# Moving the product of open attention steps ahead of a step's other VectorE work, and their bounds to GpSimd

## What is computed

```python
x = x + attn(layernorm(x)); x = x + ffn(layernorm(x))
# attn, 16 heads of 16
q_h, k_h, v_h = exp_map(q), exp_map(k), exp_map(v)          # points in the Poincare ball
diff  = |q_h|^2 - 2 q_h.k_h + |k_h|^2
denom = max((1 - c|q_h|^2) * (1 - c|k_h|^2), 1e-5)
arg   = max(1 + 2c * diff / denom, 1 + 1e-5)
w     = softmax(-beta * arccosh(arg) / sqrt(c))
out   = exp/log maps of (w @ log_map(v_h)), then @ W_o.T
# ffn: x scaled and cast to float8_e4m3, matmul with an equally cast kernel, bias
```

## Time and profile before

| what | us |
|---|---|
| median of 3 runs | 1977.56 |
| lowest, highest | 1976.21, 1979.98 |
| the profiled execution's own time | 1984.73 |
| its span, first to last instruction | 1982.9 |
| ScalarE busy | 1867.4 (94%) |
| TensorE busy | 1759.5 (89%) |
| VectorE busy | 1146.3 (58%) |
| GpSimd busy | 12.9 (1%) |
| mean granted TensorE clock | 0.974 |

### The profile page before, as it was taken

The page is one execution under the profiler, slowest core; times in us unless marked ns, Lnnn a source line. Parts: engine busy times, 40 slices in busy tenths (PEclk is TensorE's granted clock), DMA queues, the critical chain, the costliest instruction groups (busy, mean ns, idle before and its releaser), DMA issues.

```text
span 1982.9 us, 29304 instructions
## 1 busy us (share of the span) xinstructions
PE 1759.5 (89%) x10579; PEld 577.9 (29%) x10579; DVE 1146.3 (58%) x2855; ACT 1867.4 (94%) x1094; POOL 12.9 (1%) x35
## 2 busy tenths in 40 slices
PE   7989989899898798989898898998989899899896
PEld 4322222222222222222222222222222222223234
DVE  7555565655656656565656656556565655513545
ACT  5899999999999699999997899999999999999993
POOL 2000000000000000000000000000000000000000
PEclk9899999999999899999998899999999999989998
DMA  1322222041403114032040320414032031401110
GB/s 56 113 95 65 89 102 75 23 134 44 134 22 102 53 44 133 23 102 75 23 133 22 102 75 27 129 43 134 22 102 76 23 123 43 124 22 43 43 54 23
DMA packets 112952, 142.52 MB, mean 72 GB/s; under 512 B 35691, under 2 KB 61548, under 8 KB 112748
## 3 DMA queue, kind: packets, MB, share of 16 engines
q1 hardware_dynamic: 112748, 140.13, 22.8%
HBM read 85.07 MB, written 55.05 MB: 71 GB/s over the span
## 4 chain that ended last, share of the span: by engine, by line
ACT 53%; PE 24%; issue 14%; DVE 6%; ACTq 2%; DMA 0%; DVEq 0%; SPq 0%
ACT U L1217 27%; ACT U L1224 25%; PE ps L1100 8%; PE ps L402 7%; PE ps L1115 6%; ACTq L1265 2%; DVE U L1294 1%; PE ps L407 1%; DVE U L1285 1%; PE ps L698 0%; PE ps L1138 0%; ACT e L530 0%; DVE rows L555 0%; DMA U<-in_L_attn_W_o_dram 0%; DVE rp L624 0%
## 5 line engine op out<-in xcount | busy, mean ns | idle before, releaser
L1224 ACT ACTIVATE U<-U 128x2048 f32<-128x2048 f32 x512 | 1003.1, 1961 | 0.3
L1217 ACT ACTIVATE U<-ps 128x2048 f32<-128x2048 f32 x500 | 961.9, 1924 | 29.0 <-PE ps L1100 26.8
L1100 PE MATMUL ps<-q_T,k_T 18*128 18x512 f32 x4096 | 635.9, 650 | 150.2 <-ACT U L1217 113.1
L1115 PE MATMUL ps<-U,vals 128*32 128x512 f32 x4096 | 559.4, 619 | 25.7 <-ACT U L1224 24.7
L1100 PEld LDWEIGHTS ps<-q_T,k_T 18*128 18x128 f32 x4096 | 199.8, 186 | 377.4 <-ACT U L1217 316.8
L402 PE MATMUL ps<-wT,xnT 128*128 128x384 f32 x512 | 228.4, 538 | 1.9 <-ACT xnT L463 1.9
L491 DVE COPY qkv<-ps 128x384 f32<-128x384 f32 x112 | 62.5, 558 | 244.2 <-PE ps L402 244.2
L1115 PEld LDWEIGHTS ps<-U,vals 128*32 128x32 f32 x4096 | 81.5, 109 | 200.9 <-ACT U L1224 168.2
L402 PEld LDWEIGHTS ps<-wT,xnT 128*128 128x128 f32 x512 | 79.4, 190 | 193.4 <-issue 121.1
L407 PE MATMUL ps<-ident,rows 128*128 128x128 f32 x512 | 107.6, 308 | 15.9 <-DVE rows L555 13.1
L407 PEld LDWEIGHTS ps<-ident,rows 128*128 128x128 f32 x512 | 55.0, 147 | 193.6 <-issue 132.6
(11 more groups left out here) (210 smaller groups left out, 1181.6 us busy)
## 6 DMA issues: line engine op xcount, KB each, us to landing
rqb<-q_scratch SPq DMA_DIRECT2D x64, 1024.0 KB, 5.6
q_scratch<-q_T SPq DMA_DIRECT2D x16, 1024.0 KB, 4.5
k_scratch<-k_T SPq DMA_DIRECT2D x16, 1024.0 KB, 7.2
v_scratch<-vals SPq DMA_DIRECT2D x16, 768.0 KB, 4.2
fi_xt<-in_L_attn_x_dram SPq DMA_DIRECT2D x17, 512.0 KB, 5.7
xt<-in_L_attn_x_dram SPq DMA_DIRECT2D x15, 512.0 KB, 6.4
out_dram<-fi_x SPq DMA_DIRECT2D x15, 512.0 KB, 4.2
rk_scratch<-rk SPq DMA_DIRECT2D x16, 32.0 KB, 8.8
```

Of the source, the lines that this page charges most:

```text
L1100: ins = pe.matmul(g.ps[:, 2 * pair + i, :], a.k_T[HB * h:HB * h + RD, b % 2, hg, kt * P:(kt + 1) * P], a.q_T[HB * h:HB * h + RD, G % 3, hg ...
L1115: ins = pe.matmul(g.ps[HB * h:HB * h + VW, 6, :], a.vals[:, b % 2, kt, (hg * HPG + h) // 2, DH * (h % 2):DH * (h % 2) + VW], U[:, n % RING ...
L1217: act.activation(U[:, n % RING].rearrange("p b n -> p (b n)"), chunk(n), ACT.Ln, scale=-2.0 / EPS, bias=1.0).then_inc(freed, 1)
L1224: act.activation(U[:, n % RING], U[:, n % RING], ACT.Exp, scale=exponent).then_inc(exp_done, 1)
```

## The change

GpSimd now walks the 128 units with a branch of its own. In an open unit it makes the bounds of the four steps (four instructions of 128x512 each), each step as soon as its `U` buffer is free; in a closed one it adds to `m_rdy`. VectorE no longer makes bounds. Its pieces are written as `rest(n)` and now run one step later in its stream: the product of step n, then the pieces of n-1. The flag of the next unit is loaded into a register at the last step of a unit, ahead of the pieces of the step before, and only the branch stays at the unit's head. In the tables A0 goes from slot 27 to slot 26 and A1 from slot 31 to slot 32, with R1, R2, R5 and R6 whole or split to fit; in slot 25 `amax` comes ahead of the scaling of the k rows. TensorE's and ScalarE's code is otherwise the same.

```diff
-                ("R", 0): (25, BOTH), ("R", 1): (26, BOTH), ("R", 2): (27, 0), ("A", 0): (27, 1),
-                ("R", 3): (28, BOTH), ("R", 4): (29, BOTH), ("R", 5): (31, 0), ("A", 1): (31, 1),
-                ("R", 6): (32, BOTH), ("R", 7): (33, BOTH)}
+                ("R", 0): (25, BOTH), ("R", 1): (26, 0), ("A", 0): (26, 1), ("R", 2): (27, BOTH),
+                ("R", 3): (28, BOTH), ("R", 4): (29, BOTH), ("R", 5): (31, BOTH),
+                ("R", 6): (32, 0), ("A", 1): (32, 1), ("R", 7): (33, BOTH)}
...
         if k == 25:
+            v.tensor_reduce(amax[:, :], a4[:, :, :].rearrange("p t h -> p h t"), AX.X, ALU.max).then_inc(amax_rdy, 1)
             scale_rows(v, n, (1,))
-            v.tensor_reduce(amax[:, :], a4[:, :, :].rearrange("p t h -> p h t"), AX.X, ALU.max).then_inc(amax_rdy, 1)
...
+                def bound(n):
+
+                    G, hg, kt = split(n)
+                    if n >= RING:
+                        pool.wait_ge(pv_done, n - RING + 1)
+                    for h in range(HPG):
+                        ins = pool.tensor_scalar(U[:, n % RING, place(n, h), :], rqb[:, h, :],
+                                                 a.rk[:, (G // 2) % 2, hg * HPG + h, kt:kt + 1],
+                                                 1.0 / EPS, ALU.mult, ALU.min)
+                    ins.then_inc(m_rdy, 1)
+
+                for n0 in range(0, N, UNIT):
+                    o = opened(n0)
+                    pool.wait_ge(a.open_rdy, flags_of(n0))
+                    hold(pool, passed_pool)
+                    is_open = pool.value_load(a.opens[0:1, o:o + 1], min_val=0, max_val=1)
+                    with pool.If(is_open > 0):
+                        pool.wait_ge(rqb_in, 16 * (n0 // KT + 1))
+                        for n in range(n0, n0 + UNIT):
+                            bound(n)
+                    with pool.Else():
+                        if n0:
+                            pool.wait_ge(m_rdy, n0)
+                        pool.sem_inc(m_rdy, UNIT)
...
-                        if is_open and n + 1 < n0 + UNIT:
-                            bound(n + 1)
-                            clamp(n + 1)
...
+                def unit(n0, products):
+
                     for n in range(n0, n0 + UNIT):
...
+                        if products:
+                            clamp(n)
+                        if n == n0 + UNIT - 1 and UNIT <= n < N - 1:
+                            load_flag(n + 1)
+                        if n:
+                            rest(n - 1)
+                        if n == UNIT - 1:
+                            load_flag(n + 1)
```

## The result

| | before | changed |
|---|---|---|
| median of 10 runs, us | 1983.38 | 1992.88 |
| lowest, highest | 1976.21, 1989.13 | 1992.45, 1997.40 |
| the profiled execution | 1984.73 | 1992.56 |
| its span | 1982.9 | 1990.7 |

The changed kernel is slower: ratio 1.0046, 95% interval 1.0028 to 1.0064. The forecast was 32.5 us faster, with a range of 1939 to 1958 us. The time moved the other way. Of the 47.8 us between the forecast and the measured median 5.8 are this difference of the starting point; the other 42.0 are the change, 32.5 of gain that did not come and 9.5 of loss.

The account below looks back on a forecast made before the run. ScalarE, busy 94%, was taken to bound the kernel. Gains of 13.5 + 12.0 + 2.7 + 4.3 = 32.5 us off a median of 1977.56 gave 1945.1 us, main range 1939 to 1953, 8 in 10 range 1939 to 1958.

Parts of the forecast that it names:

- What bounds the kernel: ScalarE, busy 94% of the span, sets the pace; reordering other engines can only take back its idle time.
- the bound on GpSimd: Open units: 0.8 us assumed per bound of 512 elements, costing nothing up to 1.18 us because the ring covers it.
- The fourth rival: The change does nothing: bounds take about 2 us each, only the closed-unit gain is left; 1973 to 1978 us, chance 0.04.
- the slower rival: GpSimd's bounds decide the open units: slower from 2.05 us each, 2023 us at 3 us each; chance 0.06.
- Terms 1 and 2: First and second open units: earlier products cut ScalarE's waits for products and distances; gains 13.5 and 12.0 us.
- Halved waits for distances: Beside the open units, ScalarE's waits for distances of 2.6, 1.9 and 0.7 us fall to 1.3, 1.0 and nothing.
- Term 3: Third open unit: without bounds on VectorE every product is early, so waits of 2.0 and 0.7 us go; gain 2.7 us.
- Term 4: Closed units, branch at s 20: moved branch and earlier flag load remove three ScalarE waits for distances; gain 4.3 us.
- Edits at nothing: Other unit heads, A0 a step earlier, bursts of `rqb` loads and GpSimd's closed-unit branches were expected to cost nothing.
- The first: Rival: waits return inside the open units as copies behind the product delay TensorE's fill and next distances; 1956.5 us, chance 0.10.
- The second: Rival: TensorE's idle time ahead of R0 goes but one ahead of A0 comes, no closed-unit gain; 1949.4 us, chance 0.08.
- The third: Rival: VectorE pieces with two SBUF inputs wait for GpSimd bounds in units one and two, 5 us; 1950 us, chance 0.06.

Follow-up runs that it names:

- e5: Kernel before plus 32 extra GpSimd instructions of several forms behind the last values, to price them; the bounds' form took 1.99 us, no kernel time given.
- e4: Changed kernel with two heads of each open step bounded by GpSimd and two by VectorE; 1961.45 us, ratio to before 0.9887.
- e8: Changed kernel with GpSimd only multiplying, by tensor_tensor, and the minimum taken in VectorE's product; 1966.88 us, ratio to before 0.9925.
- e1: Changed kernel with the bounds back on VectorE, each step's four just ahead of its product; 1969.0 us, ratio to before 0.9927.
- e6: e2 with the first product of a unit behind the pieces, as in the kernel before; 1970.83 us, ratio to before 0.9939.
- e7: e4 with the slots of the kernel before; 1963.64 us, ratio to before 0.9900.
- e9: e8 with the slots of the kernel before for R1, A0, R2, R5, A1, R6; 1969.29 us, ratio to before 0.9930.
- e2: e1 with the slots of the kernel before for R1, A0, R2, R5, A1, R6; 1964.31 us, ratio to before 0.9917.

## Why the prediction was wrong, point by point

**What bounds the kernel** held: ScalarE is at 94% in every version, and the result followed its waits.

**The step that failed** is the bound on GpSimd, taken at 0.8 us from a memset and a select, with both ends of its range (0.45 and 1.18) below the 1.99 measured. Neither of those rows does what a bound does. The kernel before had a GpSimd tensor_scalar, the 16 instructions of L359 at 388 ns each, which the prediction doesn't use. With 16 elements a row it is nearly all fixed cost by e5's line (0.29 us fixed) and could not have given the price of 512; that had to be measured. e5 shows the form itself to be dear. The threshold that I had worked out, 1.19 us each for the first unit to be covered, was not measured itself, but fits: GpSimd spent 1.04 us per head and step in e4 and 0.98 in e8, and no product waited for it; at 2.03 eleven of twelve did.

**The fourth rival** described what came in units one and two: with 1.96 us as the price at which nothing changes, their waits rose by 1.1 and 1.3 us only. It had a chance of 0.04. Its arithmetic for the third unit, and that of the slower rival, was wrong: I gave all three units the 31.3 us of the first. In the second and the third, the values that free the first buffer and the fourth product stood like this in the kernel before:

```profile
1063.17 1.06 PE L1115 MATMUL ps<-U,vals 128*32 128x512 f32 x8
...
1095.69 2.29 DVE L1294 TENSOR_TENSOR U<-U,ps 128x2048 f32<-128x2048 f32 x1
...
1862.53 1.07 PE L1115 MATMUL ps<-U,vals 128*32 128x512 f32 x8
...
1882.79 2.29 DVE L1294 TENSOR_TENSOR U<-U,ps 128x2048 f32<-128x2048 f32 x1
```

That leaves 1095.69 - 1064.23 = 31.5 us in the second, but 1882.79 - 1863.60 = 19.2 us in the third, 1.20 each. All 48 bounds have 31.3 + 31.5 + 19.2 = 82.0 us before they make the fourth products later. At 2.01 us each (32.17 / 16) that is an estimated 14.5 us more, and 15.2 were measured. If 4.3 us come back elsewhere, "slower" begins at (82.0 + 4.3) / 48 = 1.80 us by the same estimate, not at the 2.05 that I named.

**Terms 1 and 2**, the order, held in their form once the bounds were off GpSimd. With VectorE's 1.67 us per step put back into the same steps, I expected 19 us of waits and e1 has 19.5; e6 puts the product's place at 8 to 9 us of waits. The sum as predicted, with bounds that cost neither engine anything, was never reached: e4 comes nearest with 13.2 us of waits in place of 5, so the 32.5 us are not shown for any kernel that was run.

**Halved waits for distances** next to the open units did not come true: 1.8, 3.1 and 2.1 us in the changed kernel, where I had 1.3, 1.0 and nothing.

**Term 3**, the third unit, came true where GpSimd's work stayed inside its lead: in e4, e7, e8 and e9 ScalarE waits for nothing there. In the changed kernel it was a loss of 12.7 us for products and 1.4 for distances.

**Term 4** had the mechanism right and its size from one execution. TensorE's wait for the q rows fell from 13.1 us to 2.0, and no trace with the moved branch has ScalarE's event at s 23. But "the waits are the same in each" execution, on which the sum rests, was wrong: the three events with the steps behind them are 5.5 us in the trace of before, and e5's trace of the same code has 1.9. That the branch and flag, not the slots, brought TensorE's wait down is shown by e2 and e6; which of the two, the branch behind a waiting copy or the load a step earlier, was not tried apart.

**Edits at nothing** held as far as ScalarE shows: from 1120 to 1860 us of the changed kernel it waits for nothing, in spite of the bursts of `rqb` loads.

**The rivals.** The first (waits come back inside the units) is not what held the units up: in e1 no product sat idle for TensorE. One copy did, 1.20 us in the first unit, and the product behind it was 3.78 us late where e2 has 2.50. The second (A0 takes R0's place) is refuted by the changed kernel: apart from the 4.3 us in the second open unit, TensorE's waits ahead of A0 are some 0.2 us each, and no ScalarE wait follows in closed groups. The third (the engines block each other) was small in the changed kernel, L785 568 ns where 482 were in the same stretch before, L741 637 where 195 were, L738 and L555 unchanged; e8 shows it large with another form. The Trainium skill, SBUF — State Buffer, section "Who interferes with whom", has VectorE instructions with two SBUF inputs contend with GpSimd's reads: e8 agrees with its 2.85 us for L738, while the changed kernel shows none of it for L738 with its 1.22 us and little for L785. L741, with one input, was slowed in both.

## What to carry to other kernels

Before moving work to an idle engine, take its price there from a row with the same form of instruction at a like size, and not from the cheapest rows of that engine; if there is none, measure it first. Look at what runs beside it too, since a form that is cheap there may slow the engine that was to be relieved. Work out for each place how long the receiving engine may take, place by place, since the one that hides the work best today has the least room. A wait that one trace shows in single places may be absent from the next execution of the same kernel, so it is no sure gain. Handing over half of the work may keep the gain that handing over all of it loses, and a branch or flag load is best put in front of an instruction that waits anyway.

## What the runs showed of the hardware

- On GpSimd, 512 f32 elements on 128 partitions cost 0.71 us as copy, 1.18 as tensor_tensor, 1.72 to 1.79 as tensor_scalar with one operation and 1.98 to 1.99 with two, whether the scalar is immediate or per partition. VectorE makes the last in 0.42 us (four in 1.67).
- While GpSimd ran two-input tensor_tensor instructions of 128x1024, 1.96 us each in the mean,, VectorE's neighbours grew from 1.22 to 2.85 us and from 0.28 to 1.98 (L738, L618, two f32 inputs) and from 0.20 to 1.32 (L741, one small input). While it ran tensor_scalar, L738 grew by 0 in the changed kernel and by 0.18 in e4, L741 by 0.44 us.
- Either engine can be the one that is held up. In the second unit of e8 L555 began at 1079.57 and kept its 1.22 us; GpSimd's two multiplications from 1079.89 took 4.50 us, where two took 3.75 us at 657.88.
- A flag load and a branch cost VectorE 1.0 to 1.6 us where nothing hid them (1.13, 1.04 and 1.56 in the kernel before). With both moved in front of pieces that wait for TensorE, TensorE's wait for these rows was 2.0 us in e2 and 1.8 in e6 over the whole run, where 13.1 were.
- ScalarE's single waits for distances in closed groups differ between executions of the same code: 9.2 us in the trace of before, 2.8 in e5's. TensorE ran at its lower clock for part of such a stretch: the granted clock was 0.69 from 600 to 610 us of before, around the wait that ends at 603.15.
